# Causal mask inside the score stacks, and a new order of norm, route, projections and FFN in an adaLN block

## The reference, cut to what matters

```python
h = layernorm(x) * (1 + ca) + sa
q, k, v = (lora_linear(h, w, a, b) for each)              # 16 heads of 16
scores = q @ k.T / 4;  scores = where(tril, scores, -inf) # 1024 x 1024 per head
x = x + ga * lora_linear(softmax(scores) @ v, wo, ao, bo)
h = layernorm(x) * (1 + cb) + sb
w = top-2 of softmax(h @ Wg.T + bg) over 4 experts
x = x + gb * sum_e w_e * (relu(h @ Wi.T + lora_e(h)) @ Wo.T)   # F = 1024
```

## Time and profile before

| | |
|---|---|
| median of 3 runs | 2132.53 us (2131.65 to 2134.89) |
| the profiled execution's own time | 2129.05 us |
| its span | 2127.3 us |
| mean granted TensorE clock | 0.957 of 2.4 GHz |
| instructions | 31511 |

### The profile page before, as it was taken

One profiled execution on the slowest core, in us unless ns is written; L12 is line 12 of the kernel. 1 busy time (PEld: TensorE's weight loads), 2 busy tenths in 40 slices (PEclk: granted clock), 3 DMA queues, 4 the chain that ended last, 5 costly groups with the idle time before them and its releaser, 6 DMA issues.

```text
span 2127.3 us, 31511 instructions
## 1 busy us (share of the span) xinstructions
PE 1889.3 (89%) x11124; PEld 978.3 (46%) x11124; DVE 1219.6 (57%) x2729; ACT 943.9 (44%) x1701; POOL 489.7 (23%) x791
## 2 busy tenths in 40 slices
PE   7699887999889997999979999799988999799858
PEld 5233443545335453454534454354533545343535
DVE  3767585555755566555665558555575555654142
ACT  2256553454444544444444444345444454444321
POOL 3122112222122312222122221222212231122213
PEclk9899998999899998999999999999989999899979
DMA  5413221212201122021211212121220112110100
GB/s 169 84 51 72 71 69 45 68 33 66 80 10 61 31 66 80 16 70 33 68 60 34 68 30 71 45 68 34 65 80 8 63 31 66 31 38 3 36 0 20
DMA packets 103024, 111.37 MB, mean 52 GB/s; under 512 B 20084, under 2 KB 96976, under 8 KB 102872
## 3 DMA queue, kind: packets, MB, share of 16 engines
q1 hardware_dynamic: 102856, 109.34, 18.1%
q10 hardware_dynamic: 16, 0.02, 0.0%
HBM read 75.20 MB, written 33.57 MB: 51 GB/s over the span
## 4 chain that ended last, share of the span: by engine, by line
PE 72%; DVE 14%; ACT 6%; issue 4%; SPq 2%; DMA 2%; POOL 1%; ACTq 0%; POOLq 0%; DVEq 0%
PE ov L768 11%; PE dense L848 11%; PE st L753 10%; PE mxs L739 10%; PE dense L859 5%; PE dense L825 5%; PE dense L783 5%; PE dense L833 4%; DVE negm L1139 3%; PE dense L724 3%; ACT probs L907 2%; PE mxs L743 2%; SPq L580 1%; PE dense L850 1%; DVE negm_left L1139 1%
## 5 line engine op out<-in xcount | busy, mean ns | idle before, releaser
L907 ACT ACTIVATE probs<-st 128x512 f32<-128x512 f32 (+1 forms) x1216 | 669.2, 575 | 653.8 <-PE st L753 644.1
L1139 DVE TENSOR_REDUCE negm<-mxs 128x1 f32<-128x384 f32 (+4 forms) x736 | 427.0, 615 | 212.7 <-PE mxs L743 209.6
L739 PE MATMUL mxs<-k_st,q_st 96*128 96x512 bf16 (+3 forms) x1536 | 469.7, 333 | 65.6 <-DVE negm L1139 59.4
L753 PE MATMUL st<-q_st,k_st 98*128 98x512 bf16 (+3 forms) x1536 | 452.8, 334 | 56.6 <-DMA q_st<-m_row 40.8
L1139 DVE TENSOR_REDUCE negm_left<-mxs 128x1 f32<-128x512 f32 x512 | 335.3, 685 | 139.8 <-PE mxs L739 138.7
L768 PE MATMUL ov<-probs,v_g 128*32 128x512 f32 (+3 forms) x3072 | 331.2, 501 | 19.5 <-POOL probs L633 18.7
L739 PEld LDWEIGHTS mxs<-k_st,q_st 96*128 96x128 bf16 x1536 | 149.4, 98 | 333.2 <-DVE negm L1139 181.6
L848 PE MATMUL dense<-c_t,wi_t 128*128 128x512 f32 x512 | 246.8, 604 | 3.9 <-ACT ratio_b L957 3.7
L753 PEld LDWEIGHTS st<-q_st,k_st 98*128 98x128 bf16 x1536 | 139.3, 99 | 240.4 <-ACT probs L907 92.4
L646 POOL TENSOR_TENSOR hid<-hid,second 128x512 f32<-128x512 f32 x128 | 159.7, 1270 | 294.1 <-DVE second L1207 293.5
L630 POOL TENSOR_TENSOR fence<-fence 128x1 f32<-128x1 f32 x256 | 49.9, 195 | 668.0 <-ACT probs L907 667.8
(11 more groups left out here) (162 smaller groups left out, 1680.8 us busy)
## 6 DMA issues: line engine op xcount, KB each, us to landing
q_st<-q_parts_scratch SPq DMA_DIRECT2D x384, 64.0 KB, 2.8
k_st<-k_parts_scratch SPq DMA_DIRECT2D x384, 64.0 KB, 2.9
q_parts_scratch<-q_part SPq DMA_DIRECT2D x16, 768.0 KB, 3.3
k_parts_scratch<-k_part SPq DMA_DIRECT2D x16, 768.0 KB, 4.9
xin<-in_L_attn_x SPq DMA_DIRECT2D x9, 1024.0 KB, 5.5
x<-in_L_attn_x SPq DMA_DIRECT2D x8, 1024.0 KB, 5.6
out_x<-ob SPq DMA_DIRECT2D x64, 128.0 KB, 1.7
q_st<-m_row SPq DMA_DIRECT2D x128, 4.0 KB
```

Of the source, the lines that this page charges most:

```text
L739: last = nc.tensor.matmul(mxs[:, bank_m, j * n:(j + 1) * n], q_st[0:KS, slot, h0 + j, qt * P:(qt + 1) * P], k_st[0:KS, slot, h0 + j, k0:k0 ...
L753: last = nc.tensor.matmul(st[:, score_bank(ch, kt, h0), j * n:(j + 1) * n], k_st[0:KS + 2, slot, h0 + j, kt * P:(kt + 1) * P], q_st[0:KS + ...
L907: nc.scalar.activation(probs[:, par, h0:h0 + heads, 0:n], st[:, score_bank(ch, kt, h0), 0:heads * n].rearrange("p (j q) -> p j q", q=n), A ...
L1139: nc.vector.tensor_reduce(dst[:, h0:h0 + heads], src, axis=AX.X, op=ALU.max, negate=True).then_inc(max_free, 1)
```

## The change

The mask. The causal mask moves into rows 96 to 127 of the stacks: five pairs of rows that hold powers of two make, for a query and a key of the same block, a large negative number where the key comes later and nothing that matters elsewhere. A diagonal tile's last 128 columns are now one matmul over all 128 rows; the columns before them one over 96 rows. L743, its constant tile and its matmul are gone. As rows 96 and 97 hold the maxima between times, each bundle `rs` begins with one more DMA that blanks them for its half. POOL builds the rows once at the start.

The order. Each norm is cut into 4 pieces of statistics and 7 of the rest, the route into 6. `chains` puts them at given units, up to three to a unit, between the unit's row maxima: the second norm in units 5 to 8, the route in 11 to 13, the first norm in 13 to 16 (0 to 3 in the first body). `t2` stands at 8.5 to 9.25, `rt`, `rx` at 10, `t1` at 17, the `pj` at 18 to 36, the two `ps` at 28 and 39, the `vp` at 33 to 40, and the FFN is spread from 14 to 47. A filler that may not stand yet no longer holds up others, and FFN and `vp` steps are put off when a unit has its share of what is left; the others stand at once. POOL does its part of a `pj` behind the next `qk`.

```diff
@@ pe_cost
-        return (max_keys(qt, chunk) + P * (qt // 4 == chunk)) * heads / 2.4
+        return max_keys(qt, chunk) * heads / 2.4
@@ body_plan
+    def spread(first, last, steps):
+        queue.extend((first + (last - first) * i / len(steps), (s,)) for i, s in enumerate(steps))
     if post:
+        put(OP_AT - 1, ("ce", GROUPS - 1, 1), *[("ct", i) for i in range(4)])
+        spread(OP_AT, OP_AT + 2.5, [("op", i) for i in range(4)])
+        chains += norm_steps("2", NORM2_AT)
+        spread(T2_AT - 0.5, T2_AT + 0.5, [("t2", i) for i in range(4)])
+        put(T2_AT + 1, ("rt",), ("rx",))
+        chains += [(ROUTE_AT + i // 2, ("ro", i)) for i in range(ROUTE_PARTS)]
+        put(FFN_AT, *[("mt", v) for v in range(2)], *[("rb", half) for half in range(2)])
...
+        queue.extend((FFN_AT + (FFN_END - FFN_AT) * sum(cost[:i]) / sum(cost), q) for i, q in enumerate(ffn))
     if pre:
+        t1_at = T1_AT if post else 4
+        chains += norm_steps("1", t1_at - 4)
+        put(t1_at, *[("t1", i) for i in range(4)], ("xin",))
+        spread(t1_at + 1, 28, early[:4])
+        put(28, ("ps", 0, 0))
+        spread(28, 39, early[4:])
+        put(39, ("ps", 1, 0))
+        spread(V_FREE, V_NEEDED - 2, late)
+    queue.sort(key=lambda item: item[0])
...
+        spent = unit_cost[k] + sum(map(pe_cost, mx + pinned))
+        goal = ahead / (GROUPS * NU - u)
+        ready = [q for at, q in queue if at <= u]
+        for q in ready:
+            due = u == GROUPS * NU - 1 or q[0][0] not in ("fa", "wa", "vp") or q[0] in late and u == V_NEEDED - 1
+            full = full or spent + sum(map(pe_cost, q)) / 2 > goal
+            if full and not due:
+                continue
+            fillers.append(q)
...
+        beside = [s for at, s in chains if at == u]
+        turns += [((i + 0.6) / len(beside), 3, s) for i, s in enumerate(beside)]
@@ new
+OP_AT = 2
+NORM2_AT = 5
+T2_AT = 9
+ROUTE_AT = 11
+FFN_AT = 14
+FFN_END = 47
+T1_AT = 17
+def norm_steps(which, first):
+    steps = [("ls" + which, i) for i in range(STAT_PARTS)] + [("ln" + which, i) for i in range(NORM_PARTS)]
+    return [(first + (i + 1) // 3, s) for i, s in enumerate(steps)]
@@ sync, rs
+                    sp.wait_ge(blank_out, 16)
+                    sp.wait_ge(ones_ready, 1)
+                    sp.dma_start(q_st[KS:KS + 2, slot, :, cols], blank_d.rearrange("r (j n) -> r j n", j=HG)
+                                 ).then_inc(stack_in[slot][half], 16)
@@ gpsimd, start
+            for i in range(ROW_QUERIES):
+                weight = 2.0 ** (ROW_BITS * (2 - i))
+                row_link(nc.gpsimd.affine_select(out=q_rows, in_=q_rows, compare_op=ALU.not_equal, fill=weight,
+                                                 base=first - i, pattern=[[1, P]], channel_multiplier=-ROW_QUERIES))
...
+            for stack, rows in ((q_st, q_rows), (k_st, k_rows)):
+                row_link(nc.gpsimd.tensor_copy(
+                    stack[KS:P, :, :, :].rearrange("p s j (t n) -> p (s j t) n", n=P),
+                    rows.unsqueeze(1).broadcast_to([P - KS, 2 * HG * T, P])))
@@ gpsimd
-            walk(pool, NB, run)
+            walk(pool, NB, run, late="pj", passes=POOL_IDLE, until="qk")
@@ tensor, mx
+                    left = n - P if qt // 4 == chunk else n
                     for j in range(heads):
-                        last = nc.tensor.matmul(mxs[:, bank_m, j * n:(j + 1) * n],
-                                                q_st[0:KS, slot, h0 + j, qt * P:(qt + 1) * P],
-                                                k_st[0:KS, slot, h0 + j, k0:k0 + n], start=True, stop=True)
-                        if qt // 4 == chunk:
-                            last = nc.tensor.matmul(mxs[:, bank_m, (j + 1) * n - P:(j + 1) * n], ident_b[:, :],
-                                                    causal_b[:, :], start=False, stop=True, skip_group_check=True)
+                        if left:
+                            last = nc.tensor.matmul(mxs[:, bank_m, j * n:j * n + left],
+                                                    q_st[0:KS, slot, h0 + j, qt * P:(qt + 1) * P],
+                                                    k_st[0:KS, slot, h0 + j, k0:k0 + left], start=True, stop=True)
+                        if left < n:
+                            last = nc.tensor.matmul(mxs[:, bank_m, j * n + left:(j + 1) * n],
+                                                    q_st[:, slot, h0 + j, qt * P:(qt + 1) * P],
+                                                    k_st[:, slot, h0 + j, qt * P:(qt + 1) * P],
+                                                    start=True, stop=True)
```

More of the change, by code:

```diff
@@ L124, in body_plan @@
[L124 to L148, removed]
@@ new lines, in body_plan @@
+        chains += norm_steps("2", NORM2_AT)
[3 more added lines that the diff above has]
+        put(FFN_AT, *[("mt", v) for v in range(2)], *[("rb", half) for half in range(2)])
+        ffn = []
+        for half in range(2):
+            ffn += hidden_quads(half) + [(("wa", half, t), ("w", half, t)) for t in range(4)]
+        cost = [sum(map(pe_cost, q)) for q in ffn]
@@ L171, in body_plan @@
         mx = [("mx", (g + 1) % 2, *s) for s in max_steps()[first:first + row_maxima[k]]] if more else []
[L172 to L177, removed]
-            fillers.append(queue[0][1])
-            spent += sum(map(pe_cost, queue.pop(0)[1]))
+        ahead = sum(unit_cost[v % NU] for v in range(u, GROUPS * NU))
+        ahead += sum(pe_cost(("mx", 0, *s)) for s in max_steps()) * (GROUPS - g - (not lead))
+        ahead -= sum(pe_cost(("mx", 0, *s)) for s in max_steps()[:first]) * more
+        ahead += sum(pe_cost(s) for _, q in queue for s in q)
+        spent = unit_cost[k] + sum(map(pe_cost, mx + pinned))
+        goal = ahead / (GROUPS * NU - u)
+        ready = [q for at, q in queue if at <= u]
+        full = False
+        for q in ready:
[4 more added lines that the diff above has]
+            fillers.append(q)
+            spent += sum(map(pe_cost, q))
+        queue = [(at, q) for at, q in queue if q not in fillers]
         following = []
@@ L195, in body_plan @@
                 plan.append(("ms",))
-        if parts_left and u >= 2 * NU and not any(s in early for _, q in queue for s in q):
-            plan.append(("ps", 1))
-            parts_left = False
         plan.append(("pv", g % 2, c, kt))
@@ L274, in tallied @@
         names.append("qk diagonal")
+    if step[0] in ("ln1", "ln2") and step[1] == NORM_PARTS - 1:
+        names.append("normed")
+    if step[0] in ("ls1", "ls2") and step[1] == STAT_PARTS - 1:
+        names.append(step[0] + " all")
+    if step == ("ro", ROUTE_PARTS - 1):
+        names.append("routed")
     if step[0] == "rs":
@@ L297, in with_banks, with walk @@
     return steps, n % 2
-def walk(eng, batches, run, late=None):
+def walk(eng, batches, run, late=None, passes=(), until=None):
     counts = {}
@@ L314, in done @@
                 return now.get(name, 0)
-            if held_back and s[0] not in ("mx", "pv", "qk"):
+            if held_back and s[0] not in passes:
                 run(*held_back.pop())
@@ L320, in phase @@
                 run(s, done, it, bank)
-                if held_back and s[0] == "mx":
+                if held_back and s[0] == until:
                     run(*held_back.pop())
@@ L557, in run @@
                 elif kind == "ps":
[L558 to L559 removed]
+                    ot, later = a
+                    sp.wait_ge(part3_ready, done("pj") - later)
                     for s in range(2):
                         for half in range(2):
[L562 removed]
+                            after(sp, stack_in[s][half], done(f"rs{s}{half}") * ((2 * SPLIT + 1) * 16))
                     for dst, src in ((q_d, q_part), (k_d, k_part)):
```

266 lines of the change are left out of this document (156 added, 110 removed).

## The result

The changed kernel takes 2075.59 us (median of 4 runs, 2072.05 to 2076.49) against 2133.71 for the kernel before in the same comparison: a ratio of 0.9725, with a 95% interval from 0.9708 to 0.9742. The forecast was 2057, with 2025 to 2085 as its own range. The profiled execution took 2072.05 us with a span of 2070.3 and a mean granted clock of 0.960.

A forecast was written before the change was run, and what follows sets the result against it. TensorE's stream was taken as the bound, with holes in each body's first quarter behind VectorE chains. Six bodies -66, first -7, last -4, prologue +1.5, epilogue 0: -75.5, so 2057 us, range 2025 to 2085.

The forecast's parts named there:

- Prologue, +1.5: Kernel start: 1.0 us for two maxima waiting on blanking bundles, 0.5 (between 0 and 17) for POOL's set-up.
- First body, -7: First of eight bodies, only the first norm: a hole of 7 us and its slow clock, partly given back to VectorE.
- The first quarter, 87.2 to 60.6: A body's first 14 units, summed by the slower engine: 59.1 us plus 1.5 for one low-clock spell, against 87.2.
- The rest, 165.8 to 181.2: Units 14 to 47: 165.8 us plus projections 13.8, transposes 1.8 and first norm 4.0, less 4.0 of mask: 181.2.
- 4.0 more: First norm's pieces in units 15 and 16, without FFN work, VectorE having more work than TensorE: 4.0 us added.
- Six bodies, -66: The six full bodies: each 241.8 us in place of 253.0, 11 less, so -66 us together.
- Mask, 4.0 per body: Causal columns no longer computed twice: of 4.7 us outside the first quarter, 4.0 saved per body (between 0 and 4.7).
- Last body -4 and epilogue 0: Kernel end: last body gains 4 us, having no following batch; epilogue nothing, same chain with nothing to hide it.
- (1): Rival: pieces hide better, falling where VectorE waits anyway; 7 us less per body, 2008 us; chance 0.20.
- (2): Rival: pieces only move the hole, TensorE waiting for every piece; -4 us per body, about 2100 us; chance 0.17.
- (3): Rival: TensorE at 1.2 GHz becomes the bound in units 5 to 16; 15 us more in seven bodies, 2162; chance 0.08.
- (4): Rival: planner and pieces leave the quarter as long as it was, mask's columns were hidden; 2132 us; chance 0.05.

The follow-up runs named there:

- the fastest kernel: The changed kernel with the stacks' fills by DMA instead of POOL copies and the first norm's transposes at unit 25 in place of 17: 2049.56 us, ratio 0.961.

## Why the prediction was right or wrong

**Prologue, +1.5: wrong, +14.6** (first product with V, 93.8 to 108.4). The step that failed was "POOL is free at 38.5 where its first work waits at 38.0: 0.5 us, and between 0 and 17". The copies were even cheaper than taken, 7.0 us for 10.2. The 1.25 ns per element divided the whole duration of a select of 512 and so held its fixed part. The two selects of the earlier trace rows, 0.29 us for 128 elements and 0.638 for 512, give 0.91 ns per element and 0.17 us fixed, so by estimate 7.6 us for 8192. But what failed is that I asked only who waits for POOL's result, not what POOL holds while it works. The cost stood on VectorE, and the upper end of 17 covered it by luck.

**First body, -7: wrong, -1.1** (175.2 to 174.1 from the first product with V to the first load). The mask alone gives 1.3 there and the order alone takes 3.2 (178.4). The term at fault is the hole of 7 us, which I priced in full. What took its place stays open: no run separated it.

**The first quarter, 87.2 to 60.6: right**, 60.6 in the fourth body. By parts: units 0 to 4 22.8 for 21.9, 5 to 8 20.5 for 19.6, 9 and 10 9.0 for 7.0, 11 and 12 5.4 for 5.8, 13 3.0 for 4.8, and the 1.5 of clock lies within these. That the sum is met to the tenth is luck, as units 9 and 10 are 2.0 over and unit 13 is 1.8 under. Taking the slower engine unit by unit was sound, with VectorE at 98% in units 5 to 8. TensorE, which I put at 60% there, shows 81%: 16.62 us at a clock of 0.83, where the fastest kernel has it busy for 13.89 (69%) at 1.00. No idle piece of TensorE in these units is longer than 0.91 us, and yet the clock fell. The rule that I weighed (the Trainium skill, TensorE: Matmul & The Clock Gate, Why this matters for your kernels) speaks of gaps between bursts; by its letter the low level should have gone with the long gaps, and it did not. Another section of the page (A second HAM failure mode: psum-queue depth-cycling) says that frequent small idle pieces between groups of matmuls make the clock go to and fro as well. The 0.83 of the row of units 5 to 8 fits that one, but doesn't prove it: in the fastest kernel the same units have idle pieces of up to 1.12 us at a clock of 1.00, and the clock is at its lower level only behind them, from 795.1. The sign "clock 0.98 or more in the body" failed narrowly: 0.97 in the fourth.

**The rest, 165.8 to 181.2: 183.6**, so 2.4 too little. The sum is also off by itself: its terms give 181.4. And the body had been cut by time and not by units: by units the old body was 90.1 and 162.8, and the rest grew by 20.8, just past the 20 that I had named as the mark of an error. The terms add up to a growth of 15.6, so they miss 5.2, and the base of 165.8 in place of 162.8 hid 3.0 of it. The term at fault is the "4.0 more" for the first norm and nothing for the route's end. TensorE waits 2.05 for the route's result and 2.19 for the normed rows in the timeline above, with maxima between. Setting the norm later returned 1.7 per body; for the rest of the 5.2 no run gives the place.

**Six bodies, -66: -47.5.** Forecast 11 each, measured 7.9; the fourth is among the better, at 8.8 from load to load.

**Mask, 4.0 per body: right**, 4.4 alone (4.0 with the fills by DMA) and 5.0 with the order.

**Last body -4 and epilogue 0: wrong, -23.0.** The step that failed was "the last body has no following batch". But it has a second norm, a route and an FFN as the others do, and loses the same two holes. From the seventh load to the last product with V, and from there to the end, before and after:

```profile
1784.10:2007.90 223.80, 196.23 (x1178) 97.61 (x1170) 109.56 (x240) 102.01 (x185) 49.52 (x86) 0.95 0.12 32
2007.90:2127.30 119.40, 89.61 (x337) 56.92 (x334) 35.93 (x99) 19.29 (x31) 25.71 (x24) 0.84 0.03 9
```

```profile
1750.10:1954.60 204.50, 187.60 (x1140) 92.93 (x1140) 106.34 (x236) 100.80 (x184) 48.10 (x83) 0.97 0.10 28
1954.60:2070.30 115.70, 85.64 (x334) 53.87 (x334) 36.02 (x100) 19.09 (x31) 26.45 (x25) 0.88 0.07 22
```

The last body gives 19.3 of the 23.0, its idle TensorE time falling from 27.6 to 16.9 us. That it gains more than a full body because no projections come back later is argued, not shown. In one go instead of pieces the two stretches together take 9.3 us more. In the epilogue TensorE is busy for 4.0 us less with the same work, at a clock of 0.88 for 0.84.

**The sum.** The start was forecast 19.0 too low, the six bodies 18.5 too low and the end 19.0 too high. The last of these hid one of the other two, so that the total came within 18.5 us is in part luck.

**The rivals.** (1) did not come: pieces weren't hidden in VectorE's idle time beyond the forecast. (2), that pieces only move the hole, is near for the second norm, where pieces gain 1.6 of 22.1 us, and wrong for the others. (3) did not come: the clock is 0.92 over the quarter, at the lower level part of the time, and units 5 to 8 took 0.4 us more with it than without. (4) fell with the quarter's 60.6 us and the mask alone, 21.6 us less.

## What to carry to other kernels

Of a step off the critical path ask not only who waits for its result but which engine it holds up while it works: long fills on GpSimd belong where VectorE is idle, or on a DMA. Cutting a chain into pieces and moving the work that used to cover it are two changes with opposite signs, here about 9 and 6 us per body; price each. Where an engine is full over a whole stretch, moving its work inside the stretch renamed the wait or made it longer.

## What was not expected of the hardware

A VectorE operation of 0.18 us took 6.95 beside a memset on GpSimd in which it has no part, and short fills stretched many operations (0.68 to 1.40) where long ones stopped two. GpSimd's copy of 8192 bf16 elements from rows read over and over took 7.01 us, hardly more than a memset of the same length, 6.92: 0.86 ns per element, where its select of 512 has 1.25 over its whole duration. Two DMAs that write 480 KB each in pieces of 256 bytes landed 6.1 and 8.8 us after their issue, and nobody waited for them.
